# A look-ahead of seven groups in place of fourteen for the gathers of a three-layer graph network kernel

## The chip, the cores and the metric

One Trainium2 chip, one of its cores. The metric is the device time of one execution in microseconds (us), as the median of several runs. The engines are TensorE (PE), VectorE (DVE), ScalarE (ACT), GpSimd (POOL) and SyncE (SP). Every engine runs its own list of instructions; they meet at semaphores.

## The reference

A graph of 3125 nodes with 128 features and 53125 arcs (each node has one to itself; the kernel calls a node's number of arcs its degree) goes three times through this layer, and then through a last normalization:

```python
msg = concat([h[src], h[dst]]) @ Mw.T + Mb
s1, s2 = segment_sum(msg, dst), segment_sum(msg * msg, dst)
mx, mn = segment_max(msg, dst), segment_min(msg, dst)
mean = s1 / deg;  var = relu(s2 / deg - mean * mean);  std = sqrt(var + 1e-30)
agg = concat([mx, mn, std, var])
u = concat([h, agg, agg * (logd / 4), agg * (4 / logd)]) @ Uw.T + Ub
u = batch_norm(u / sqrt(N));  h = leaky_relu(u @ mix_w.T + mix_b) + h
h = elu(layer_norm(h))
...
out = layer_norm(x + h)
```

Only h[src] @ part of Mw has to be fetched for each arc. The kernel stores that product and its square, p and p*p, as a table in memory with one row of 1 KB for each node, and for each node gathers the rows of its sources, from which come sum, sum of squares, largest and smallest.

## The kernel before, in words

**Prologue.** Degrees are counted on TensorE, nodes are ranked by degree, and the indices of each node's sources are laid out by rank, so that each of the 25 tiles of 128 nodes has nodes of nearly one degree. The first table (`p_by_node`) is stored by node, and a second (`p_by_rank`) by rank. In `project(-1, c)` TensorE makes the products of seven chunks of four tiles (the last has one), VectorE adds the bias (L1440), ScalarE squares (L1058), and SyncE stores the chunk (L561). Before those stores SyncE issues 36 small transfers that fill `shared_index` (L557).

**Stage A of a layer** is where the change is. A slot is one gathered row for each of a tile's 128 nodes: one indirect DMA of GpSimd, of 128 rows (L742). Up to four slots are a group; `GROUPS` is the list of the 112 groups of a layer in order, and `own_slots[n]` says how many of group n's slots GpSimd gathers itself: 387 a layer, 1161 in all. Groups 0 to 3 (`AHEAD`) hold two slots for each of eight late tiles, 4 and 5 are tile 0, 6 to 8 tile 1, 9 to 11 tile 2, and so on. Before group 9, GpSimd gathers ten more sets of rows into `shared` (L727), out of which SyncE fills a few single slots by its own transfers (`shared_rows`, L564 to L585). Groups 26, 35 and 44 hold only such slots.

The gathered groups lie in a ring `G` of `R` = 14 places of four slots. Group n lies at place n % 14. Who uses a group:

- VectorE, `accumulate(l, n)`: adds, takes the larger and takes the smaller into PSUM, three instructions a group (L1470 to L1472). The last of them counts up `dve_used` ("groups_compared"). A tile's first group (j = 0) is copied by ScalarE instead (`begin`, L1101 to L1103), and is counted together with the tile's second. The AHEAD groups go into `base` (L1488 to L1490).
- ScalarE, in the first layer alone, `keep_ranks(l, n)` (L1091): writes the gathered rows' ranks back into `index`, and counts `rank_kept`.

At a tile's end VectorE reduces (`close`, L1692 to L1696), ScalarE squares the mean (`square_mean`, L1109), VectorE takes the variance (L1714), ScalarE the root (L1116), TensorE turns the aggregates (L921) and multiplies (L933, L936), ScalarE copies (L1129, L1135, L1141), and VectorE combines (L1722, L1724).

**What sets GpSimd's order.** `gather(l)` goes through the groups in order; its gathers are issued one after another and land by themselves. From group 14 on it first waits until VectorE has used the group that lay at this place, and in layer 0 until ScalarE has kept its ranks. GpSimd can thus be at most fourteen groups ahead. In layers 1 and 2 the first four groups wait for as many chunks of the new table as they need, and group 4 for all of it. Each further group wait on SyncE's side (L575) goes by R too.

**What VectorE waits for before its first group.** `take_ahead` waits for `base_ready`: ScalarE's `bases(l)` must have copied and scaled all tiles' own rows (L1075, L1077, and in layers 1 and 2 L1074), which begins when the last chunk has been squared. In layer 0 it waits also for the seven stores of `p_by_rank` (`s_firstp`).

**Stage B of a layer** (batch norm, mix, layer norm, ELU, next table) runs chunk by chunk on TensorE, ScalarE and VectorE, when the last tile is done. After layer 2 GpSimd scatters the outputs (L753).

Of the kernel before, what the change touches and what calls it, by code (L numbers as in the profile page):

```python
# [72 lines left out]
def build(nc, x, src, dst, w_p, b_p, w_q, w_h, w_u, w_mix, v_cols, out):  # L73
# [101 lines left out]
            GROUPS.append((T - 1, -1, 0, hi - lo))  # L175
    NG = len(GROUPS)
    R = 14
    W = 2 * D + 1
    slot_before, slot_total = [], [0] * R
    kept_to = [sum(k > 0 for k in own_slots[:n + 1]) for n in range(NG)]  # L180
    for n in range(NG):
        slot_total[n % R] += 16 * own_slots[n]
        slot_before.append(slot_total[n % R])
    tile_groups = [[n for n, g in enumerate(GROUPS) if g[0] == t and g[1] >= 0] for t in range(T)]
# [13 lines left out]
    with ctx:  # L198
        def sb(name, shape, dt=FP32):
            return ctx.enter_context(nc.sbuf_tensor(name, shape, dt))  # L200

        def sem(name):
            return ctx.enter_context(nc.semaphore(name))
# [4 lines left out]
        rank_dram = nc.dram_tensor("rows_by_rank", [NP, RW], FP32).ap()  # L208
        p0_table = nc.dram_tensor("p_by_node", [NP, W], FP32).ap()
        p_table = nc.dram_tensor("p_by_rank", [NP, 2 * D], FP32).ap()  # L210
# [36 lines left out]
        shared_index = sb("shared_index", [P, NOV, 2], I32)  # L247
        shared = sb("shared_rows", [P, NOV, W])
        rdeg = sb("rdeg", [P, T])
# [10 lines left out]

        G = sb("G", [P, R, GW, W])
        G_flat = G[:, :, :, :].rearrange("p r k f -> p (r k f)")

        def carver(flat, size):
            taken = [0]

            def carve(n):
                at = taken[0]
                taken[0] += n
                assert taken[0] <= size  # L270
                return flat[:, at:at + n]

            return carve
# [12 lines left out]

        carve = carver(G_flat, R * GW * W)
        hot_lo = carve(P * HC)[0:EP, :].bitcast(BF16).rearrange("p (b j c) -> p b j c", b=2, c=HC)
# [3 lines left out]
        digit_b = carve(EC)[0:EP, :].bitcast(BF16).rearrange("p (b c) -> p b c", b=2)  # L292
        carve = carver(G_flat, R * GW * W)
        p_nat = carve(T * W).rearrange("p (t f) -> p t f", f=W)
        rows_flat = carve(T * RW)
# [132 lines left out]
        dve_used = Signal(sem("groups_compared"), NG)  # L428
        rank_kept = Signal(sem("ranks_kept"), NG)
# [181 lines left out]
        def _(pool):  # L611
# [66 lines left out]
            def extras(l):  # L678

                with pool.If(pool.value_load(extra_i[0:1, T:T + 1], min_val=0, max_val=T * E) > 0):  # L680
                    with pool.Fori(0, T) as t:
                        more = pool.value_load(extra_i[0:1, bass.ds(t, 1)], min_val=0, max_val=T * E)
                        with pool.If(more > 0):
                            with pool.Fori(0, more):
                                pool.wait_ge(x_arc, 1)
                                pool.sem_clear(x_arc)
                                g.indirect_dma_start(ex_src[:, :], None,
                                                     src.rearrange("(e a) -> e a", a=1),
                                                     bass.IndirectOffsetOnAxis(ap=ex_arc[:, :], axis=0))\
                                    .then_inc(x_src, 16)  # L690
                                pool.wait_ge(x_node, 1)
                                pool.sem_clear(x_node)
                                g.indirect_dma_start(ex_row[:, :], None, p0_table,
                                                     bass.IndirectOffsetOnAxis(ap=ex_node[:, :], axis=0))\
                                    .then_inc(x_p, 16)
                                if l:
                                    pool.wait_ge(x_rank, 1)
                                    pool.sem_clear(x_rank)
                                    g.indirect_dma_start(ex_row[:, 0:2 * D], None, p_table,
                                                         bass.IndirectOffsetOnAxis(ap=ex_rank[:, :], axis=0))\  # L700
                                        .then_inc(x_q, 16)
                        pool.nop()
                    pool.nop()
                pool.nop()

            def gather(l):

                if l:
                    pool.wait_ge(s_need, 1)
                    needs = [pool.value_load(need_i[0:1, l - 1, a:a + 1], min_val=p_stored.at(l - 1, 16),  # L710
                                             max_val=p_stored.at(l - 1, 16 * NC)) for a in range(len(AHEAD))]
                for n, (t, ahead, k0, _) in enumerate(GROUPS):
                    table, w = (p_table, 2 * D) if l else (p0_table, W)
                    if l and n in AHEAD:
                        pool.wait_ge(p_stored.sem, needs[n])
                        pool.sem_inc(s_turn, 1)
                    elif n == len(AHEAD) and l == 0:
                        pool.wait_ge(s_infor, 80)
                    elif n == len(AHEAD):
                        pool.wait_ge(p_stored.sem, p_stored.at(l - 1, 16 * NC))  # L720
                    if n == tile_groups[2][0]:
                        if l == 0:
                            pool.wait_ge(s_sidx, 16 * len(PARTS))
                        if l == 1:
                            pool.wait_ge(s_skept, 1)
                        for c in range(NOV):
                            g.indirect_dma_start(shared[:, c, 0:w], None, table,  # L727
                                                 bass.IndirectOffsetOnAxis(ap=shared_index[:, c, 0:1], axis=0))\
                                .then_inc(shared_in.sem, 16)
                    if n == R:  # L730
                        if l == 0:
                            pool.wait_ge(s_extra, 1)
                            pool.sem_inc(s_turn, 1)
                        extras(l)
                    if n >= R:

                        pool.wait_ge(dve_used.sem, dve_used.at(l, n - R + 1))
                        if l == 0:
                            pool.wait_ge(rank_kept.sem, rank_kept.at(l, kept_to[n - R]))
                    for j in range(own_slots[n]):  # L740
                        named = index[:, t + j, k0:k0 + 1] if n in AHEAD else index[:, t, k0 + j:k0 + j + 1]
                        g.indirect_dma_start(G[:, n % R, j, 0:w], None, table,  # L742
                                             bass.IndirectOffsetOnAxis(ap=named, axis=0))\
                            .then_inc(gathered[n % R].sem, 16)
# [3 lines left out]
            for l in range(L):  # L748
                gather(l)
# [1122 lines left out]
```

## Time and profile before

| what | value |
|---|---|
| median of 3 runs | 1751.79 us (1750.67 to 1752.85) |
| span of the profiled execution | 2141.7 us |
| GpSimd busy, of the span | 1235.7 us (58%) |
| VectorE busy | 1096.6 us (51%) |
| TensorE busy (matmul) | 682.6 us (32%) |
| ScalarE busy | 455.6 us (21%) |
| gathers of L742 | 1161, 949 ns each |

The profiled execution is 389.9 us (22%) longer than the median of the timed runs; of its own time only the span is given. A busy share is the time in which instructions of that engine ran, out of the span. For GpSimd a gather's duration is the issue, and not the transfer, which goes on behind it. The stretches by layer, by the first and the last gather: layer 0 from 110.8 to 708.5 us, layer 1 from 784.0 to 1378.0, layer 2 from 1450.5 to 2029.4; what lies before is the prologue, between them stage B, and behind them stage B and the output.

### The profile page before, as it was taken

How to read it: one execution, taken by the hardware profiler on the slowest of the kernel's cores; microseconds unless marked ns; L12 is line 12 of the kernel's file. 1: busy time of each engine (PE TensorE's matmuls, PEld its weight loads, DVE VectorE, ACT ScalarE, POOL GpSimd, SP SyncE). 2: the span in 40 equal slices, each digit the busy share in tenths (PEclk: the TensorE clock that was granted, in tenths of full speed). 3: DMA queues.
4: the chain of work that ended last, by engine and by line, in shares of the span. 5: the costliest groups of instructions: out<-in, count | busy, mean ns of one | idle time of the engine just before them, and what ended most of it. 6: DMA issues, size and time to landing. Idle time of an engine off the chain costs nothing. (4 is left out here: it accounts for less than half of the span.)

```text
span 2141.7 us, 10446 instructions
## 1 busy us (share of the span) xinstructions
PE 682.6 (32%) x2156; PEld 402.8 (19%) x2156; DVE 1096.6 (51%) x2178; ACT 455.6 (21%) x1024; POOL 1235.7 (58%) x1358
## 2 busy tenths in 40 slices
PE   5611233132322470323132232362113322233265
PEld 5311121011111230112111111131101211112122
DVE  8600755464644843445464463572525664466464
ACT  0103321122111154111111111136101221112125
POOL 7673666676666127745675675406756666576504
PEclk9975666565655685566565666686556666656677
DMA  4363333333333033323332232204323333333200
GB/s 59 105 167 113 93 103 103 91 99 92 92 91 91 18 112 113 111 66 99 96 101 76 88 103 75 65 27 145 106 84 101 93 88 93 88 103 96 76 0 30
DMA packets 97107, 190.18 MB, mean 89 GB/s; under 512 B 30792, under 2 KB 56984, under 8 KB 97040
## 3 DMA queue, kind: packets, MB, share of 16 engines
q0 software_dynamic: 59968, 160.78, 26.6%
q1 hardware_dynamic: 37077, 28.77, 4.9%
q14 instruction: 47, 0.39, 0.1%
q8 instruction: 15, 0.25, 0.0%
HBM read 168.75 MB, written 17.75 MB: 87 GB/s over the span
## 5 line engine op out<-in xcount | busy, mean ns | idle before, releaser
L742 POOL DMA_INDIRECT G<-p_by_rank,index x774 | 734.8, 949 | 560.2 <-issue 227.8
L742 POOL DMA_INDIRECT G<-p_by_node,index x387 | 367.4, 949 | 225.0 <-issue 120.3
L921 PE MATMUL ps<-wide_ident,agg 128*128 128x128 f32 x288 | 80.3, 434 | 1209.3 <-issue 701.2
L1470 DVE TENSOR_TENSOR ps<-ps,G 128x1024 f32<-128x1024 f32 (+3 forms) x222 | 250.3, 1127 | 191.2 <-issue 78.4
L921 PEld LDWEIGHTS ps<-wide_ident,agg 128*128 128x128 f32 x288 | 51.5, 217 | 1239.5 <-issue 721.9
L936 PE MATMUL ps<-w_u_sb,aggT 128*128 128x384 f32 x576 | 284.3, 654 | 0.0
L1714 DVE SCALAR_TENSOR_TENSOR var<-tot,rdeg,msq 128x128 f32<-128x128 f32 x75 | 26.1, 348 | 426.4 <-ACT msq L1109 407.8
L936 PEld LDWEIGHTS ps<-w_u_sb,aggT 128*128 128x128 f32 x576 | 162.6, 282 | 144.7 <-issue 119.1
L1135 ACT ACTIVATE u_sb<-ps 128x128 f32<-128x128 f32 x75 | 20.7, 277 | 721.1 <-remote 509.0
L1472 DVE TENSOR_TENSOR ps<-ps,G 128x512 f32<-128x512 f32 (+3 forms) x222 | 141.6, 638 | 0.0
L1471 DVE TENSOR_TENSOR ps<-ps,G 128x512 f32<-128x512 f32 (+3 forms) x222 | 141.5, 637 | 0.0
L933 PE MATMUL ps<-w_own,hT 128*128 128x384 f32 x144 | 107.3, 849 | 4.1 <-remote 2.0
L1692 DVE TENSOR_REDUCE tot<-ps 128x256 f32<-128x1024 f32 x72 | 88.2, 1225 | 34.6 <-remote 21.6
L1129 ACT ACTIVATE aggT<-ps 128x512 f32<-128x512 f32 x72 | 42.3, 587 | 245.8 <-remote 171.7
L1109 ACT ACTIVATE msq<-tot,rdeg 128x128 f32<-128x128 f32 x75 | 29.8, 397 | 244.0 <-DVE tot L1692 177.3
L1101 ACT ACTIVATE ps<-G 128x1024 f32<-128x1024 f32 x72 | 72.8, 1011 | 1.8 <-issue 1.8
L753 POOL DMA_INDIRECT out_h<-G,index x25 | 24.8, 993 | 80.4 <-ACT G L1215 72.8
L1488 DVE TENSOR_TENSOR base<-base,G 128x1024 f32<-128x1024 f32 x12 | 14.8, 1233 | 76.9 <-remote 67.2
L1141 ACT ACTIVATE uT<-ps,v_sb 128x128 f32<-128x128 f32 x75 | 27.4, 365 | 115.2 <-remote 75.5
L839 PE MATMUL ps<-w_p_sb,hT 128*128 128x128 f32 x150 | 26.5, 331 | 77.4 <-issue 51.6
L1116 ACT ACTIVATE agg<-agg,eps_std 128x128 f32<-128x128 f32 x75 | 30.1, 401 | 90.2 <-DVE agg L1717 60.0
L1696 DVE TENSOR_REDUCE agg<-ps 128x128 f32<-128x512 f32 x72 | 49.0, 681 | 0.0
(280 smaller groups left out, 1328.3 us busy)
## 6 DMA issues: line engine op xcount, KB each, us to landing
G<-p_by_rank,index POOLq DMA_INDIRECT x774
p_by_rank<-base SPq DMA_DIRECT2D x18, 512.0 KB
G<-p_by_node,index POOLq DMA_INDIRECT x387
p_by_node<-G SPq DMA_DIRECT2D x6, 514.0 KB
w_u_sb<-in_w_u SPq DMA_DIRECT2D x3, 768.0 KB
x_r<-rows_by_rank SPq DMA_DIRECT2D x1, 1600.0 KB
G<-shared_rows SPq DMA_DIRECT2D x12, 53.0 KB
windows<-src_pad SPq DMA_DIRECT2D x1, 624.8 KB, 14.1
```

Of the source, the lines that this page charges most:

```text
L742: g.indirect_dma_start(G[:, n % R, j, 0:w], None, table, bass.IndirectOffsetOnAxis(ap=named, axis=0))\
L921: ins = nc.tensor.transpose(ps[:, 2, i * D:(i + 1) * D], agg[:, t % 2, i * D:(i + 1) * D], ident[:, :])
L933: mm(z, hT[:, hot(t)], w_own[:, :], start=True, stop=False)
L936: ins = mm(z, aggT[:, t % 2, i * D:(i + 1) * D], w_u_sb[:, i, :], start=False, stop=i == 3)
L1101: f(run, G[:, n % R, :, 0:2 * D], ACT.Copy)
L1116: f(agg[:, t % 2, 2 * D:3 * D], agg[:, t % 2, 3 * D:4 * D], ACT.Sqrt, bias=eps_std[:, 0:1]).then_inc(std_ready.sem, 1)
L1129: f(aggT[:, t % 2, :], ps[:, 2, :], ACT.Copy).then_inc(agg_copied.sem, 1)
L1470: TT(run[:, 0:nk, :], run[:, 0:nk, :], G[:, n % R, 0:nk, 0:2 * D], ALU.add)
L1471: TT(top[:, 0:nk, :], top[:, 0:nk, :], here, ALU.max)
L1472: TT(low[:, 0:nk, :], low[:, 0:nk, :], here, ALU.min).then_inc(dve_used.sem, 2 if j == 1 else 1)
L1692: sums = v.tensor_reduce(tot[:, t % 2, :], run.rearrange("p k f -> p f k"), AX.X, ALU.add)
L1696: least = v.tensor_reduce(agg[:, t % 2, D:2 * D], low.rearrange("p k d -> p d k"), AX.X, ALU.min)
```

## The change

GpSimd waits from group 7 on for the group seven back, in place of from group 14 on for the group fourteen back. The ring keeps its 14 places, and SyncE's wait for its own slots still goes by R.

```diff
     R = 14
+    LOOK = 7
...
-                    if n >= R:
-
-                        pool.wait_ge(dve_used.sem, dve_used.at(l, n - R + 1))
+                    if n >= LOOK:
+
+                        pool.wait_ge(dve_used.sem, dve_used.at(l, n - LOOK + 1))
                         if l == 0:
-                            pool.wait_ge(rank_kept.sem, rank_kept.at(l, kept_to[n - R]))
+                            pool.wait_ge(rank_kept.sem, rank_kept.at(l, kept_to[n - LOOK]))
```

No instruction of another engine moves or changes. On GpSimd waits are added at the start of each layer. The list of GpSimd at the start of layer 0's gathers, before; `G<-p_by_node,index` is a gather of L742, and the first two rows are groups 0 to 3, the next two groups 4 to 8:

```order
L742 DMA G<-p_by_node,index 128x257 [waits first_p_stored,indices_of_early_tiles_loaded]
L742 DMA G<-p_by_node,index 128x257 x15
L742 DMA G<-p_by_node,index 128x257 [waits indices_by_rank_loaded]
L742 DMA G<-p_by_node,index 128x257 x17
L727 DMA shared_rows<-p_by_node,shared_index 128x257 [waits shared_index_loaded]
L727 DMA shared_rows<-p_by_node,shared_index 128x257 x9
L742 DMA G<-p_by_node,index 128x257 x17
```

The same place with the change (line numbers are one higher):

```order
L743 DMA G<-p_by_node,index 128x257 [waits first_p_stored,indices_of_early_tiles_loaded]
L743 DMA G<-p_by_node,index 128x257 x15
L743 DMA G<-p_by_node,index 128x257 [waits indices_by_rank_loaded]
L743 DMA G<-p_by_node,index 128x257 x11
L743 DMA G<-p_by_node,index 128x257 [waits ranks_kept,groups_compared]
L743 DMA G<-p_by_node,index 128x257
L743 DMA G<-p_by_node,index 128x257 [waits ranks_kept,groups_compared]
L743 DMA G<-p_by_node,index 128x257 x3
L728 DMA shared_rows<-p_by_node,shared_index 128x257 [waits shared_index_loaded]
L728 DMA shared_rows<-p_by_node,shared_index 128x257 x9
L743 DMA G<-p_by_node,index 128x257 [waits ranks_kept,groups_compared]
L743 DMA G<-p_by_node,index 128x257 x3
```

The first wait for VectorE and ScalarE stands now behind 28 gathers (16 and 12) instead of behind 51 gathers and the ten of L728, and the ten stand behind two such waits.

The start of layer 1, with the change; before, the row x11 was x17 and led without a wait up to the ten shared gathers:

```order
L743 DMA G<-p_by_rank,index 128x256 [waits p_stored]
L743 DMA G<-p_by_rank,index 128x256 x11
L743 DMA G<-p_by_rank,index 128x256 [waits groups_compared]
L743 DMA G<-p_by_rank,index 128x256
L743 DMA G<-p_by_rank,index 128x256 [waits groups_compared]
L743 DMA G<-p_by_rank,index 128x256 x3
L728 DMA shared_rows<-p_by_rank,shared_index 128x256 [waits shared_ranks_kept]
```

Here too group 7 is the first that waits for VectorE, and no wait for ScalarE stands beside it.

## Rows read from the trace of the kernel before

**Rows 1.** The page: span, busy time by engine, and the groups of line 742.

```profile
span 2141.7 us, 10446 instructions
PE 682.6 (32%) x2156; PEld 402.8 (19%) x2156; DVE 1096.6 (51%) x2178; ACT 455.6 (21%) x1024; POOL 1235.7 (58%) x1358
...
L742 POOL DMA_INDIRECT G<-p_by_rank,index x774 | 734.8, 949 | 560.2 <-issue 227.8
L742 POOL DMA_INDIRECT G<-p_by_node,index x387 | 367.4, 949 | 225.0 <-issue 120.3
```

**Rows 2.** Who waited for whom, GpSimd: us in total, times, longest us.

```profile
POOL G L742 <- DVE ps L1472: 175.2, 23, 23.2
...
POOL G L742 <- ACT index L1091: 77.6, 9, 32.7
POOL G L742 <- DVE ps L1587: 23.0, 2, 11.6
```

**Rows 3.** Timeline, GpSimd: start us, us, instruction, [idle before <-releaser].

```profile
110.80 0.99 POOL L742 DMA_INDIRECT G<-p_by_node,index  x1 [7.18 <-DMA index<-rows_by_rank]
...
145.87 0.94 POOL L742 DMA_INDIRECT G<-p_by_node,index  x1 [0.30 <-issue]
...
219.48 1.69 POOL L742 DMA_INDIRECT G<-p_by_node,index  x1 [32.66 <-ACT index L1091]
...
707.58 0.94 POOL L742 DMA_INDIRECT G<-p_by_node,index  x1 [2.22 <-DVE ps L1472]
...
783.97 1.11 POOL L742 DMA_INDIRECT G<-p_by_rank,index  x1 [75.45 <-DMA p_by_rank<-base]
...
819.14 0.94 POOL L742 DMA_INDIRECT G<-p_by_rank,index  x1 [0.31 <-issue]
...
1377.10 0.94 POOL L742 DMA_INDIRECT G<-p_by_rank,index  x1 [8.26 <-DVE ps L1472]
...
2028.48 0.94 POOL L742 DMA_INDIRECT G<-p_by_rank,index  x1 [0.52 <-DVE ps L1472]
```

**Rows 4.** Timeline, VectorE: first and last use of gathered groups in a layer.

```profile
216.78 1.23 DVE L1488 TENSOR_TENSOR base<-base,G 128x1024 f32<-128x1024 f32 x1 [9.68 <-ACT base L1077]
...
750.68 0.28 DVE L1583 TENSOR_TENSOR agg<-ps,G 128x128 f32<-128x128 f32 x1
...
836.69 1.23 DVE L1488 TENSOR_TENSOR base<-base,G 128x1024 f32<-128x1024 f32 x1 [34.30 <-remote]
...
1418.90 0.28 DVE L1583 TENSOR_TENSOR agg<-ps,G 128x128 f32<-128x128 f32 x1
...
2070.71 0.28 DVE L1583 TENSOR_TENSOR agg<-ps,G 128x128 f32<-128x128 f32 x1
```

**Rows 5.** Who waited for whom, VectorE's largest.

```profile
DVE var L1714 <- ACT msq L1109: 407.8, 29, 27.4
```

**Rows 6.** Timeline, ScalarE, the bases of layer 1.

```profile
810.16 1.82 ACT L1077 ACTIVATE base<-base,self_w 128x256 f32<-128x256 f32 x4
...
817.77 0.51 ACT L1077 ACTIVATE base<-base,self_w 128x256 f32<-128x256 f32 x1 [0.89 <-issue]
```

**Rows 7.** Timeline, VectorE, a tile of four groups in layer 2: its start, the next one's.

```profile
1872.24 1.23 DVE L1470 TENSOR_TENSOR ps<-ps,G 128x1024 f32<-128x1024 f32 x1 [1.68 <-ACT ps L1103]
...
1886.00 1.23 DVE L1470 TENSOR_TENSOR ps<-ps,G 128x1024 f32<-128x1024 f32 x1 [1.65 <-issue]
```

**Rows 8.** Timeline, VectorE, chunks of the table: layer 0, and the last one before layer 1.

```profile
127.11 0.69 DVE L1440 TENSOR_TENSOR base<-ps,b_p_sb 128x512 f32<-128x512 f32 x1 [8.72 <-issue]
156.41 0.69 DVE L1440 TENSOR_TENSOR base<-ps,b_p_sb 128x512 f32<-128x512 f32 x1 [28.61 <-remote]
...
196.38 0.69 DVE L1440 TENSOR_TENSOR base<-ps,b_p_sb 128x512 f32<-128x512 f32 x1 [6.37 <-remote]
...
200.29 0.89 DVE L1440 TENSOR_TENSOR base<-ps,b_p_sb 128x512 f32<-128x512 f32 x2 [1.23 <-PE ps L839]
...
799.28 0.29 DVE L1440 TENSOR_TENSOR base<-ps,b_p_low 128x128 f32<-128x128 f32 x1 [0.89 <-issue]
```

**Rows 9.** Timeline, SyncE's transfers in the prologue.

```profile
117.23 0.44 SPq L551 DMA_DIRECT2D v_sb<-in_v_cols  x1
117.72 35.15 SPq L557 DMA_DIRECT2D shared_index<-rows_by_rank  x36
```

## The prediction

> **What bounds the kernel now.** I read the page first, then GpSimd's waits, then the timelines of GpSimd and VectorE at the seams of the layers. On the page GpSimd is the busiest engine, and its gathers are 949 ns each [rows 1]. They do not follow at 949 ns: the 28 gathers from 110.80 to 145.87 us took 35.07 us, 1.25 us each, and the group's "issue" share (348.1 us of idle time before 1161 gathers, 0.30 each) is the rest of it [rows 1, 3]. The same 1.25 us stands wherever GpSimd waits for nobody. With the ten shared gathers a layer there are 3 x 397 = 1191 of them: 1489 us of GpSimd.
>
> In the profiled execution GpSimd has waits on top of that: 175.2 + 77.6 + 23.0 = 275.8 us for a ring place, released by VectorE or ScalarE [rows 2]. And VectorE is far behind: it ends its last group 43.4, 42.1 and 42.5 us after the last gather of the layer was issued [rows 3, 4]. If VectorE were close behind, some 5 us would do for the issue, the landing and the last use (an estimate: 0.94 for the issue, about 1 for the last three instructions, the rest for the landing). Three times 37.5 is 112 us. Both together, 388 us, are what the profiled execution has over a kernel that only gathers at 1.25 us without a pause. Its span is 389.9 us over the median of the timed runs: 2141.7 - 388 = 1753.7 against 1751.79.
>
> From this I take that the timed runs have none of those waits: there GpSimd issues from a layer's start to its end, and VectorE follows. VectorE can: its whole busy time is 1096.6 us [rows 1], and a tile of four groups, 15 gathers or 18.8 us of GpSimd, costs it 13.8 us when nothing holds it [rows 7]. What holds it in the profile is a stretch in which the other engines are served slowly while GpSimd gathers. ScalarE does four scalings in 1.82 us at 810.16, and from 812.9 on each of the same takes a turn of 1.40 us (0.51 busy, 0.89 "issue") [rows 6]; VectorE's 407.8 us for the squared mean are the same thing further down the chain [rows 5]. These stretches are in the profile; by the sum above they are not in the timed runs. The Trainium skill, page "NOTIFIC — the notification-queue block", section 3, says that the unit that writes trace records can push back on the engines that produce them and so stall one; no run here shows that this is the cause.
>
> **The change, part by part.**
>
> 1. *Removed:* nothing. *Added:* 28 waits in the list of GpSimd (seven more groups a layer, on two semaphores in layer 0). A wait that is already met costs nothing here: gathers with and without one before them start 1.25 us apart [rows 3]. I take 0; an upper bound of 0.02 us each is under 1 us.
>
> 2. *Start of layer 0.* GpSimd starts at 110.80 and has issued groups 0 to 6, 28 gathers, when it comes to group 7 at 145.87 [rows 3]. With the change it stands there until VectorE has used group 0 and ScalarE has kept its ranks. In the profile that is 219.48, but only because of the slow stretch: chunk 0 of the table passed VectorE at 127.11, chunk 1 at 156.41, and then, when GpSimd had paused, the chunks from 196.38 to the last (end 201.18) took 4.8 us for three steps [rows 8]. Two steps of those are 200.29 - 196.38 = 3.9 us. Without a slow stretch the six steps from 127.11 are 3 x 1.95 + 4.8 = 10.7 us, and the last chunk is through at about 137.8. From there to the first use of a gathered group it is 216.78 - 201.18 = 15.6 us (ScalarE's table load and its bases) [rows 4, 8]: 153.4. From the start of that use to GpSimd's next gather it is 219.48 - 216.78 = 2.7: 156.1. The other path is SyncE's: 36 small transfers at the 0.49 us between its rows, 17.6 us, end at 135.3 [rows 9]; the seven stores behind them then go out as their chunks come, and land beside the 15.6 us of the bases. So GpSimd stands still from 145.87 to 156.1, 10.2 us. The contention of the stores with the gathers and the first keeping of ranks will add a little; I take 12. What is queued behind the wait is everything: 23 gathers of groups 7 to 13 and the ten shared ones, 41.3 us of issue, that were already under way before. Since GpSimd sets the end of the layer, those 12 us are not given back.
>  Bounds: below, 0, if VectorE were ready by 145.87; above, 30. For that the slow stretch is there until GpSimd stops at 145.87; after it chunk 1 passes at some 147, the five steps to the last are 2 x 1.95 + 4.8 = 8.7 us, then come 15.6 and 2.7: 174, or 28 us.
>
> 3. *Start of layers 1 and 2.* Group 7 comes at 819.14, 35.2 us after the layer's first gather [rows 3]. The last chunk passed VectorE at 799.57 [rows 8]. From there it is layer 0's 15.6 us again, with one more copy a chunk (seven of some 0.6) and without the table load (some 1.3): 18.5, an estimate; then 2.7 give 820.8, and without the slow turns before 799.28 about 3 us less. A wait of 0 to 2 us each; I take 0. At the profile's own slow values it would be 836.69 + 2.7 - 819.14 = 20 us each.
>
> 4. *In the middle of the layers.* Seven places hold at least 16 gathers of GpSimd's own (13 where the group waited for is counted with the next one), 16 to 20 us. A wait there needs VectorE to be that far behind the landing. With the tail of a tile (13.8 less three groups of 2.5, about 6 us), a group of its own and the four single slots of a shared group, I come to at most some 17, and that only behind the nine shared groups. I take 0, and an upper bound of 1 us at each of the nine shared groups.
>
> Sum: 12 us over the profiled execution's figure without its waits, and so over the median: 1751.8 + 12 = 1764.
>
> **A rule that speaks for more.** The profile shows 34 ring waits, and they come back every 60 us or so [rows 2]. The Trainium skill, page "Perfetto Trace Analysis", section "Optimization Strategy", says that a gap which repeats on the engine that should be saturated can mean too few buffers. By that rule halving the lead would lengthen each gap; by the sum above there are none in timed runs to lengthen. It is the second rival.
>
> **The rivals.**
>
> - *A, the forecast:* one stop, at layer 0's start. 1757 to 1774. Chance 0.55.
> - *B, more stops:* the repeating gaps are real, in part. VectorE is as late at the starts as the profile has it, or nearly: 30 us in layer 0, and up to 20 in layers 1 and 2. From 1782 with the first alone up to 1822 with all three. For it speaks every timeline of the profile; against it that GpSimd's 1489 us and the 246 us before, between and behind the layers' uses (110.8, 33.0, 31.3 and 70.7) leave only 17 us of the median, landings included. Chance 0.2.
> - *C, nothing:* VectorE's chain, and not GpSimd, ends the layers, so that a lead of gathers that are lost at the start is not missed, or VectorE is ready before 145.87. For it speaks that in the profile VectorE is 42 us late at every end. 1751 to 1754. Chance 0.17.
> - *D, faster:* the slow stretch while GpSimd gathers is in the timed runs too, and VectorE's chain sets the end. Then the stop at 145.87 ends the slow stretch 41 us earlier than before (GpSimd's last gather before its pause began at 185.9), and VectorE begins layer 0 at 172 in place of 216.78: up to 45 us off, 1707. It decides from the point where VectorE is still more than a few us behind at 707.58, the layer's last gather. Half of the saving, lost again to a thinner lead, would be 1730. Chance 0.08.
>
> That the change would not do what it says is excluded by the list of instructions: group 7 waits in every layer.
>
> **How the numbers follow.** The likeliest case gives 1764. Its own range is 1757 to 1774. The range for 8 in 10 takes in case C and B's first step: 1751 to 1788; what is left out is D and the upper half of B, some 0.18. A measurement of this kernel can tell about 0.2%, 3.5 us, from no change. The chance of over 0.2% faster is D's, 0.08; of within 0.2% C's, 0.17; of over 0.2% slower A's and B's, 0.75.
>
> **What would show it.** In the profile with the change GpSimd's 29th gather has a gap before it that ends with VectorE's first L1491 or ScalarE's L1092, and VectorE's first use of a group lies at 150 to 180, not at 216.78. Its ring waits will be more than 34, and the longest no longer 32.7. GpSimd's pace between waits stays at 1.25 us. The timed difference should lie near 12 us and not near 40 to 70. I am wrong if the timed runs are within 3.5 us, or if they are over 1785; the first would say that GpSimd is not what ends layer 0, the second that VectorE falls back by more than 16 gathers in timed runs too.

## The result, and the profile after

| | time |
|---|---|
| before, 12 runs | 1750.34 us (1746.51 to 1752.85) |
| after, 12 runs | 1753.37 us (1752.11 to 1756.52) |
| ratio | 1.0024, 95% interval 1.0016 to 1.0032 |

The medians lie 3.0 us apart; the ratio, which uses all runs, gives 4.2 us, with an interval of 2.8 to 5.6. The forecast was 12 (1764.0, with a range of 1751 to 1788): the sign was right, the size was three to four times too large.

The page of the profiled execution after, which answers to [rows 1]:

```profile
span 1750.9 us, 10453 instructions
...
PE 670.2 (38%) x2156; PEld 394.9 (23%) x2156; DVE 1094.0 (62%) x2178; ACT 456.0 (26%) x1024; POOL 1236.1 (71%) x1358
...
L743 POOL DMA_INDIRECT G<-p_by_rank,index x774 | 736.2, 951 | 307.0 <-issue 232.4
...
L743 POOL DMA_INDIRECT G<-p_by_node,index x387 | 367.4, 949 | 128.4 <-issue 113.9
```

The busy times of VectorE, ScalarE and GpSimd are those of before within 2.6 us, and TensorE's is 12 us less, but the span is 390.8 us shorter. That is not the change: this time the profiled execution looks like the timed ones (1750.9 beside 1753.37). The slow stretches of rows 5 and 6 are gone: ScalarE's four scalings of a chunk take 1.69 us from the first to the last, and the wait for the squared mean is no longer among VectorE's largest. GpSimd's waits show the same, to be held against [rows 2] (us in total, times, longest):

```profile
POOL G L743 <- issue: 346.3, 1137, 0.3
POOL G L743 <- DMA p_by_rank<-base: 71.8, 2, 36.8
...
POOL G L743 <- DVE base L1491: 6.5, 1, 6.5
...
POOL G L743 <- DVE ps L1473: 3.7, 12, 0.3
```

The 34 ring waits of 275.8 us are one of 6.5 us. Every other gather has the 0.30 us before it that it has without a wait; the second row is the two starts of layers 1 and 2.

The one stop is where the prediction put it. GpSimd's timeline (start us, us, instruction, idle before and its releaser), at the seams of the layers:

```profile
108.22 0.99 POOL L743 DMA_INDIRECT G<-p_by_node,index  x1 [4.62 <-DMA index<-rows_by_rank]
...
142.22 0.94 POOL L743 DMA_INDIRECT G<-p_by_node,index  x1 [0.30 <-issue]
149.71 1.68 POOL L743 DMA_INDIRECT G<-p_by_node,index  x1 [6.55 <-DVE base L1491]
...
610.99 0.94 POOL L743 DMA_INDIRECT G<-p_by_node,index  x1 [0.30 <-DVE ps L1588]
...
647.02 1.10 POOL L743 DMA_INDIRECT G<-p_by_rank,index  x1 [35.09 <-DMA p_by_rank<-base]
...
682.88 1.63 POOL L743 DMA_INDIRECT G<-p_by_rank,index  x1 [0.30 <-issue]
...
1144.00 0.94 POOL L743 DMA_INDIRECT G<-p_by_rank,index  x1 [0.30 <-DVE ps L1588]
...
1679.16 0.95 POOL L743 DMA_INDIRECT G<-p_by_rank,index  x1 [0.30 <-DVE ps L1588]
```

The 29th gather starts at 149.71 instead of at 143.46: 6.25 us of stop. In layer 1 the same gather comes at 682.88 with no stop. VectorE, in the same stretches, beside [rows 4] and [rows 8]:

```profile
122.18 0.69 DVE L1441 TENSOR_TENSOR base<-ps,b_p_sb 128x512 f32<-128x512 f32 x1 [5.96 <-PE ps L840]
124.16 0.69 DVE L1441 TENSOR_TENSOR base<-ps,b_p_sb 128x512 f32<-128x512 f32 x1 [1.29 <-PE ps L840]
125.50 0.69 DVE L1441 TENSOR_TENSOR base<-ps,b_p_sb 128x512 f32<-128x512 f32 x1 [0.64 <-PE ps L840]
...
129.16 0.89 DVE L1441 TENSOR_TENSOR base<-ps,b_p_sb 128x512 f32<-128x512 f32 x2 [0.31 <-PE ps L840]
...
147.01 1.23 DVE L1489 TENSOR_TENSOR base<-base,G 128x1024 f32<-128x1024 f32 x1 [11.08 <-DMA p_by_rank<-base]
...
677.55 1.23 DVE L1489 TENSOR_TENSOR base<-base,G 128x1024 f32<-128x1024 f32 x1 [14.86 <-ACT base L1078]
...
1148.39 0.28 DVE L1584 TENSOR_TENSOR agg<-ps,G 128x128 f32<-128x128 f32 x1
...
1683.47 0.28 DVE L1584 TENSOR_TENSOR agg<-ps,G 128x128 f32<-128x128 f32 x1
```

Two things are to be seen. The last chunk is through at 130.05, and the first use of a group starts at 147.01, 38.8 us after the first gather; in the profiled execution of before it was 106.0 us after it (216.78 - 110.80). And VectorE begins its last group of layers 1 and 2 now 4.4 and 4.3 us after the last gather began (1148.39 - 1144.00 and 1683.47 - 1679.16), where before it was 42 us in both.

### The profile page after: what moved, and what is told of

Its sections match the earlier page's. It is cut to its first block and busy times, and to the rows that moved or that the text cites. A ratio compares the mean times of both kernels' runs of the same rounds, so it can differ in the third digit from the quotient of the medians.

```text
span 1750.9 us, 10453 instructions
## 1 busy us (share of the span) xinstructions
PE 670.2 (38%) x2156; PEld 394.9 (23%) x2156; DVE 1094.0 (62%) x2178; ACT 456.0 (26%) x1024; POOL 1236.1 (71%) x1358
## 5 line engine op out<-in xcount | busy, mean ns | idle before, releaser
L937 PE MATMUL ps<-w_u_sb,aggT 128*128 128x384 f32 x576 | 277.4, 641 | 0.0
L937 PEld LDWEIGHTS ps<-w_u_sb,aggT 128*128 128x128 f32 x576 | 158.8, 276 | 141.5 <-issue 113.1
L1472 DVE TENSOR_TENSOR ps<-ps,G 128x512 f32<-128x512 f32 (+3 forms) x222 | 141.3, 637 | 0.0
L1092 ACT ACTIVATE index<-G 128x4 int32<-128x4 f32 (+2 forms) x108 | 21.1, 202 | 187.2 <-DMA G<-p_by_node,index 187.2
L1697 DVE TENSOR_REDUCE agg<-ps 128x128 f32<-128x512 f32 x72 | 49.0, 680 | 0.0
L1695 DVE TENSOR_REDUCE agg<-ps 128x128 f32<-128x512 f32 x72 | 48.9, 680 | 0.0
L665 POOL DMA_INDIRECT base<-windows,row_i x25 | 37.5, 1501 | 13.7 <-issue 7.3
L1103 ACT ACTIVATE ps<-G 128x512 f32<-128x512 f32 x72 | 42.1, 585 | 0.0
```

The lines of the kernel that those rows point to most:

```text
L937: ins = mm(z, aggT[:, t % 2, i * D:(i + 1) * D], w_u_sb[:, i, :], start=False, stop=i == 3)
L1103: f(top, G[:, n % R, :, 0:D], ACT.Copy)
L1472: TT(top[:, 0:nk, :], top[:, 0:nk, :], here, ALU.max)
L1695: most = v.tensor_reduce(agg[:, t % 2, 0:D], top.rearrange("p k d -> p d k"), AX.X, ALU.max)
L1697: least = v.tensor_reduce(agg[:, t % 2, D:2 * D], low.rearrange("p k d -> p d k"), AX.X, ALU.min)
```

## The experiments

"Theory 1" in the expectations is the prediction's view with the sizes of the trace after: timed runs have no slow stretch, GpSimd's unbroken issue sets the time, and a shorter look-ahead costs its stops at the starts of the layers and nothing between them. Line numbers of a kernel with the extra lines are one higher than before, in mid3 two.

### Was the slow stretch in the kernel or in one execution?

**look14** is the kernel before, unchanged, profiled again.

> The kernel before, unchanged, for a second profile of it and for the noise of a comparison. Theory 1 (GpSimd's issue at 1.25 us a gather bounds every timed run; the stretches of slow service belonged to that one profiled execution): the span is 1746 to 1752 us, no ring wait before any gather, VectorE's first use of a group in layer 0 at 147 to 151 us, ratio 1.000. Theory 2 (a lead of fourteen groups makes the slow stretches in every profiled execution): the span is again near 2140 us with some 276 us of ring waits, ratio 1.000.

Measured: 1749.44 us beside 1749.73 for before, ratio 1.0004 (0.9992 to 1.0016). Its page, and then GpSimd's waits:

```profile
span 1747.0 us, 10446 instructions
...
PE 658.7 (38%) x2156; PEld 387.7 (22%) x2156; DVE 1094.2 (63%) x2178; ACT 456.6 (26%) x1024; POOL 1238.3 (71%) x1358
```

```profile
POOL G L742 <- issue: 349.8, 1148, 0.3
...
POOL G L742 <- ACT index L1091: 1.2, 4, 0.3
...
POOL G L742 <- DVE ps L1472: 0.9, 3, 0.3
```

The same kernel, 394.7 us shorter, and no ring wait of more than the 0.3 us of issue. Theory 1 had that right, but not VectorE's first use in layer 0: it comes at 145.15, ahead of the 147 to 151 expected. So rows 2 to 6 described one execution and not the kernel. None of the other profiles below has a slow stretch either. From here on look14 stands for the profile of before.

### Which of the added waits costs?

**only_start** has the look-ahead of seven only in layer 0's groups 7 to 13, **not_start** everywhere else.

```diff
 only_start
+                    back = LOOK if l == 0 and n < R else R
 not_start
+                    back = R if l == 0 and n < R else LOOK
 both
-                    if n >= LOOK:
-                        pool.wait_ge(dve_used.sem, dve_used.at(l, n - LOOK + 1))
+                    if n >= back:
+                        pool.wait_ge(dve_used.sem, dve_used.at(l, n - back + 1))
```

> The look-ahead of seven only in layer 0 for groups 7 to 13; fourteen elsewhere. Theory 1 (the whole price is the one stop at layer 0's group 7): same as the changed kernel, 1753 us, +2 to +4 us over before, with one ring wait of 6 to 7 us. Rival (the price is spread over the layers, in waits too short to be seen): 1750 to 1751 us.

> The look-ahead of seven everywhere but for groups 7 to 13 of layer 0. Theory 1: same as before, 1750 us, within 1 us, and no ring wait over 0.5 us. Rival (spread over the layers): +2 to +3 us.

Measured: only_start 1753.49, ratio 1.0018 (1.0006 to 1.0030); not_start 1750.97, ratio 1.0008 (0.9997 to 1.0018), both beside 1749.73. only_start has one stop, of 4.8 us where 6 to 7 were expected, and not_start none:

```profile
147.83 1.68 POOL L743 DMA_INDIRECT G<-p_by_node,index  x1 [4.79 <-DVE base L1491]
```

So the waits of layer 0's groups 7 to 13 alone cost what the whole change costs. All the other places have the shorter look-ahead in not_start, and its ratio is not distinct from 1. By the times alone they could still cost up to 3.2 us, and its median is 1.2 us up where within 1 was expected; that they cost nothing is shown by its trace, in which no gather waits for a place.

### Does the price follow the stop?

**look9**, **look6** and **look5** set `LOOK` to nine, six and five.

> Look-ahead nine in every layer. Theory 1 (the price of a look-ahead is its stop at the layers' starts, and nothing in mid-layer): the first wait stands at group 9, behind the ten shared gathers, some 57 us after the layer's first gather, when VectorE has used more than group 0 (its use ends 41 us after it in layer 0, 36 us in layers 1 and 2). No ring wait over 0.5 us, span 1745 to 1749, the median within 2 us of before's 1750. Rival (a thinner lead costs all along the layers, by late landings): about two thirds of what seven costs, 2.5 us, so 1752 to 1753.

> Look-ahead six in every layer. Theory 1: the wait at group 6 comes 3 to 5 us earlier than the one at group 7, with VectorE as late as before: stops of 10 to 11 us in layer 0 and of 3 to 4 us in each of layers 1 and 2, together 16 to 19, of which 1 to 3 come back as shorter waits behind VectorE's first instructions: a median of 1765 to 1768. Rival (only layer 0's start costs, and the other two starts have room): 10 us, 1760.

> A look-ahead of five. Theory 1, from the profile of the changed kernel: group 5 comes after 20 gathers, 25 us after a layer's first; VectorE has used group 0 at 149.4, 680.0 and 1213.9 us there, so the stops are 16, 8 and 7 us, 31 in all; with the 3 us that were missing at seven, 1778 us (1.016). If a stop is given back in about half wherever it is, 1766 us. If VectorE in the middle of a layer is further behind than five groups, there are more stops and it is over 1785 us.

Measured: look9 1749.0, ratio 1.0000 (0.9989 to 1.0010), no stop; look6 1761.57, ratio 1.0063 (1.0047 to 1.0079); look5 1778.6, ratio 1.0156 (1.0138 to 1.0174). The stops of the last two, GpSimd's waits in look6 and its timeline in look5:

```profile
POOL G L743 <- ACT index L1092: 11.9, 5, 10.6
...
POOL G L743 <- DVE base L1491: 3.4, 2, 2.7
```

```profile
148.11 1.68 POOL L743 DMA_INDIRECT G<-p_by_node,index  x1 [14.95 <-DVE base L1491]
...
690.22 1.69 POOL L743 DMA_INDIRECT G<-p_by_rank,index  x1 [7.25 <-DVE base L1491]
...
1231.91 1.69 POOL L743 DMA_INDIRECT G<-p_by_rank,index  x1 [7.92 <-DVE base L1491]
```

look9 and look5 came as theory 1 had it. look6 missed its 1765 to 1768 by 3.4 us and lay nearer to the rival's 1760: its stop in layer 0 is the expected 10.6, but those of layers 1 and 2 are 0.7 and 2.7, of which 0.3 is the normal gap, in place of 3 to 4. The rival's reason (the other two starts have room) is nevertheless wrong, since they do stop; they stop less. In layer 1 VectorE's first use comes 29.0 us after the first gather, 1.5 sooner than in after, and a gather of 1.95 us just ahead of the stop took 1.0 us of it, which the next experiment explains.

### What shortens a stop again?

In look14 the gathers beside VectorE's first instructions are not all of 0.95 us. GpSimd, then VectorE, in the same few microseconds:

```profile
145.85 1.35 POOL L742 DMA_INDIRECT G<-p_by_node,index  x1 [0.30 <-issue]
147.50 0.95 POOL L742 DMA_INDIRECT G<-p_by_node,index  x1 [0.31 <-issue]
148.75 1.43 POOL L742 DMA_INDIRECT G<-p_by_node,index  x1 [0.30 <-issue]
150.49 1.63 POOL L742 DMA_INDIRECT G<-p_by_node,index  x1 [0.30 <-issue]
```

```profile
145.15 1.23 DVE L1488 TENSOR_TENSOR base<-base,G 128x1024 f32<-128x1024 f32 x1 [9.69 <-ACT base L1077]
146.29 0.68 DVE L1489 TENSOR_TENSOR base<-base,G 128x512 f32<-128x512 f32 x1
...
147.50 1.26 DVE L1488 TENSOR_TENSOR base<-base,G 128x1024 f32<-128x1024 f32 x1
148.68 0.68 DVE L1489 TENSOR_TENSOR base<-base,G 128x512 f32<-128x512 f32 x1
149.28 0.68 DVE L1490 TENSOR_TENSOR base<-base,G 128x512 f32<-128x512 f32 x1
...
150.09 1.21 DVE L1488 TENSOR_TENSOR base<-base,G 128x1024 f32<-128x1024 f32 x1
151.22 0.68 DVE L1489 TENSOR_TENSOR base<-base,G 128x512 f32<-128x512 f32 x1
```

Take 0.95 us back from the end of each long gather: 146.25, 149.23 and 151.17, each 0.04 or 0.05 before VectorE's next instruction begins. They look held until the instruction in which they started is over: each ends 0.82 us after that instruction's end (147.20 after 146.38, 150.18 after 149.36, 152.12 after 151.30). The gather that starts together with one, at 147.50, is not held. In the eleven profiles without a slow stretch it is the same each time: 108 gathers begin at least 0.06 us inside one of the three and more than 0.14 us before its end, and all end 0.81 or 0.82 us after it; 47 begin within 0.04 us of its start, and none is held. Four gathers a layer are held in look14. Over all gathers longer than 0.96 us, what they take beyond 0.946 us (the excess, below) is 7.2 us in look14 and 6.0 in after. **light14** and **light7** are the kernels before and after without the sum and the maximum of the four early groups (two of the three instructions; their results are missing from eight tiles).

```diff
-                TT(sums, sums, G[:, n % R, :, 0:2 * D], ALU.add)
-                TT(most, most, here, ALU.max)
                 TT(least, least, here, ALU.min).then_inc(dve_used.sem, 1)
```

> The kernel before, with the sum and the maximum of the four early groups left out (their minimum alone is taken, one instruction of 0.69 us a group in place of three of 2.6). Theory P (a gather that starts while one of those instructions with both operands in SBUF runs is held until it ends: the 12 gathers of 1.35 to 1.69 us at the starts of the layers, 6.1 us over the 0.95 in all, are that): at most 0.5 us a layer of such excess is left, and the span falls by 4.5 to 6.5 us from the 1747.0 of the kernel before, to 1740.5 to 1742.5; median near 1745. Rival (the long gathers come from other traffic, such as the landing of the first transfers or SyncE's stores): the excess stays near 2 us a layer and the span near 1747.

> The same leaving out, with the look-ahead of seven. Theory P with theory 1: VectorE has used group 0 some 1.9 us sooner, so the one stop is 2.9 to 4.7 us (in place of 4.8 to 6.5), and since there are no held gathers that a stop could spare, all of it is lost: span 3 to 4.7 us over that of the same kernel with fourteen. Rival (what a stop loses comes back by some other way, as 1.3 to 2.6 us of it did with the full kernel): 1 to 2.5 us over it.

Measured, beside 1750.45: light14 1743.79, ratio 0.9967 (0.9956 to 0.9977), light7 1746.31, ratio 0.9979 (0.9968 to 0.9989). The excess is 1.8 us in light14 instead of 7.2 (0.5 to 0.7 a layer, where at most 0.5 was expected); the median fell by 6.7 us (4.0 to 7.7 by the interval). The long gathers went with the instructions, so they are VectorE's doing. The expected span, 1740.5 to 1742.5, was missed: 1745.4. Of the 5.4 us less of excess only 2.9 show in the sum of the 1191 gathers' durations (1134.0 to 1131.1), since the other gathers of that one execution were 2 ns longer each; look9's are 2 ns longer than look14's as well, though nothing there should change them, and the median of ten runs is the better witness. In light7 the stop is 3.1 us over the normal gap:

```profile
146.64 1.15 POOL L743 DMA_INDIRECT G<-p_by_node,index  x1 [3.44 <-DVE base L1489]
```

light7's median is 2.5 us above light14's, which is the upper end of the rival's 1 to 2.5. The expectation of 3 to 4.7 was for spans, and light7's span is even 1.6 us the shorter one: single spans scatter by more than what was to be told apart here. So theory P is borne out by light14, and whether something else gives part of a stop back is not settled by light7.

The Trainium skill, page "SBUF — State Buffer", section "SBUF: two separate sides", says that VectorE and GpSimd share a pair of ports which an instruction of VectorE with two inputs in SBUF can hold for its whole length against a GpSimd instruction that reads SBUF. The trace agrees: L1488 to L1490 have both inputs in SBUF, and a gather that starts inside one ends 0.82 us after it. L1470 to L1472 have one input in PSUM and run 222 times each; 398 gathers of look14 begin while one of them runs, and none takes over 0.96 us. Of the few others that are long, the first of layer 1 (1.09 us) and one in the middle of layer 2 (1.06) began inside instructions with all inputs in SBUF too (L1807, L1714), and they too end 0.82 us after them.

### What lies between the stop of 4.8 and that of 6.5?

In after VectorE's first use was released by the last store of `p_by_rank`, at 147.01, 1.4 us after ScalarE's last base (145.62). **stores_first** is the changed kernel with SyncE's seven stores ahead of the 36 small transfers.

```diff
-            sp.wait_ge(s_cleared, 1)
-            for t, _, lo, hi, q, c, o in PARTS:
...
             for c, (t0, nt) in enumerate(CH):
                 sp.wait_ge(p_copied.sem, p_copied.at(-1, c + 1))
                 sp.dma_start(p_table[t0 * P:(t0 + nt) * P, :].rearrange("(t p) f -> p t f", p=P),
...
+            sp.wait_ge(s_cleared, 1)
+            for t, _, lo, hi, q, c, o in PARTS:
```

> The changed kernel, with SyncE's seven stores of the table by rank ahead of the 36 small transfers. In the profile of the changed kernel VectorE's first use was released at 147.01 by the last of these stores, 1.4 us behind ScalarE's last base (145.62); in the one with seven at the start alone both came at 145.0 to 145.1. Theory S (the store is the later of the two in some executions and makes the stop 6.5 in place of 4.8): the first use is released by ScalarE's base, at 145.0 to 146.0, the stop is 4.7 to 5.7 us and the median falls by 0 to 1.5 us from 1753.4. Rival (the store comes late because of the gathers' traffic, and not because of its place in SyncE's list): it is still the store that releases VectorE, at 146 or later.

Measured: 1753.57, ratio 1.0020 (1.0010 to 1.0029). VectorE's first use and GpSimd's stop:

```profile
144.93 1.23 DVE L1489 TENSOR_TENSOR base<-base,G 128x1024 f32<-128x1024 f32 x1 [9.69 <-ACT base L1078]
```

```profile
147.63 1.69 POOL L743 DMA_INDIRECT G<-p_by_node,index  x1 [4.70 <-ACT index L1092]
```

As theory S had it for the trace: ScalarE's base releases VectorE and the stop is 4.7. But one profile can't show that the order did it, since six of the ten undisturbed profiles with the old order have ScalarE as the releaser too. In those ten, VectorE's first use comes 36.8 to 39.0 us after the first gather. The store is the last to come in four of them, and late by over 1 us in two, after and look9 (38.8 and 39.0); the other eight lie at 36.8 to 37.8, most of which spread is the time between the first two chunks (1.2 to 2.5 us). With the 2.7 us from there to the next gather, and GpSimd's 35.2, the ten would make stops of 4.3 to 6.5 us, 4.9 in the middle (an estimate from these rows). The median did not move by anything that can be measured, so the longer stop is not in most timed runs, or its 1.5 us are too few to see.

### Is the middle of the layers free at any look-ahead?

**mid3** leaves groups 7 to 13 alone and waits from group 14 on for the group three back.

```diff
-                    if n >= LOOK:
+                    back = R if n < R else 3
+                    if n >= back:
```

> A look-ahead of three in the middle of the layers alone: groups 14 and up wait for the group three back, groups 7 to 13 for none. From the table of when each group was gathered and used in the profile of the same kernel with fourteen: with seven, six or five no group of the middle would have to wait, with four one or three a layer, with three 17 or 18 a layer. Theory 1 (the middle costs nothing at seven because VectorE is there never more than some 14 us behind, and starts to cost where the lead falls under that): ring waits of 95 us in all if each stop also delays the uses behind it, 19 us if it delays none; a median of 1769 to 1845, and above 1765 in any case. Rival (GpSimd's gathers are hidden in mid-layer and VectorE's own work sets the pace there): under 5 us, 1755 or less.

Measured: 1839.38 us, ratio 1.0515 (1.0498 to 1.0531), 89.0 us over before. GpSimd's waits:

```profile
POOL G L744 <- DVE ps L1474: 57.5, 33, 4.9
POOL G L744 <- DVE ps L1589: 42.5, 15, 5.4
```

With ScalarE's, 46 stops of 88.0 us over the normal gap. The 95 expected if each stop also delays the uses behind it came from look14's trace, from a table of when each group was gathered and used. So the middle is not free by nature; at seven it is free because VectorE is never so far behind that group n - 7 is still in use when GpSimd comes to group n.

### All together

Stops are the idle time before gathers over the normal 0.30 us, in one profiled execution; excess is that of the long gathers, against look14's 7.2; the last column is the median's difference from before in the same series, in us.

| kernel | stops | excess against look14 | sum | measured |
|---|---|---|---|---|
| light14 | 0 | -5.4 | -5.4 | -6.7 |
| light7 | 3.1 | -4.9 | -1.8 | -4.1 |
| look9 | 0 | 0.0 | 0.0 | -1.5 |
| not_start | 0 | -1.0 | -1.0 | +1.2 |
| only_start | 4.5 | -0.1 | 4.4 | +3.8 |
| stores_first | 4.4 | -0.8 | 3.6 | +3.2 |
| after | 6.2 | -1.2 | 5.0 | +3.0 |
| look6 | 13.1 | -1.3 | 11.8 | +11.1 |
| look5 | 29.2 | -2.3 | 26.9 | +28.9 |
| mid3 | 88.0 | +0.9 | 88.9 | +89.0 |

Over a range of 90 us the stops and the held gathers account for the time within 2.4 us. Effects smaller than that this table can't tell apart: not_start has 1.0 us less excess than look14 without any stop.

## Why the prediction was right in sign and three to four times too large

**What bounds the kernel: right.** "GpSimd issues from a layer's start to its end" in timed runs was worked out from a profile that showed the opposite, as 2141.7 - 388 = 1753.7. look14 shows it directly: span 1747.0, no ring wait. The 1.25 us a gather stands in every profile, and longer stops lengthen the time one for one (look6, look5, mid3).

**Part 1, waits that are met cost 0: right.** look9 and not_start.

**Part 2, one stop in layer 0: right in place and releaser, wrong in size.** In time after the first gather:

| step | predicted | after |
|---|---|---|
| GpSimd comes to group 7 | 35.1 | 35.2 |
| first chunk at VectorE | 16.3 | 14.0 |
| from there to the end of the last chunk | 10.7 | 7.9 |
| last chunk to first use | 15.6 | 17.0 (15.6 in look14) |
| first use to the next gather | 2.7 | 2.7 |
| GpSimd goes on | 45.3 | 41.5 |
| stop | 10.2 | 6.2 |

The step that failed is "the six steps from 127.11 are 3 x 1.95 + 4.8 = 10.7", and its starting point. Both were read from rows 8. The starting point lies in the slow stretch: the chunk at 127.11 has "8.72 <-issue" ahead of it, and 16.3 us after the first gather became 14.0. The steps of 1.95 lie behind it, in GpSimd's pause (its last gather before that began at 185.9), and there VectorE waited for TensorE ("1.23 <-PE ps L839" in rows 8). The eight products of a chunk, in before and in after:

```profile
196.26 2.08 PE L839 MATMUL ps<-w_p_sb,hT 128*128 128x128 f32 x8 [25.77 <-ACT hT L1063]
```

```profile
124.40 1.06 PE L840 MATMUL ps<-w_p_sb,hT 128*128 128x128 f32 x8
```

In before TensorE had stood idle for 25.77 us, and its granted clock was 0.50 from 196 to 200 us, the 1.2 GHz level; in after it was at work since 118.11, and the clock was 1.00 from 124 to 131, the 2.4 GHz level. So behind the idle stretch the products took twice as long, and the steps read there were 1.95, where all eleven undisturbed profiles have 1.33 for the second to the fourth step (124.16, 125.50 above). The first step is of another size, 1.98 in after. Together it is 5.2 us too many (2.4 for the starting point, 2.8 for the steps), of which 1.4 came back by the late store. The prediction had SyncE's stores land beside the bases; in after the last of them landed 1.4 us behind. The two intervals that were copied whole, 15.6 and 2.7, were exact but for that store (15.6 in look14). Then "the contention ... will add a little; I take 12" added 1.8 for what was 1.4 in this execution, 0.1 in only_start and 0 in stores_first.

**"Those 12 us are not given back": not refuted, and not shown to the last us.** The stop falls where VectorE holds gathers: in layer 0 two are held by its first instructions in place of four. From the first to the last gather layer 0 takes 5.3 us more than in look14 (502.8 against 497.5), for a stop of 6.2; its excess is 0.7 us less. The excess of all three layers is 1.2 us less, but 0.5 of that is in layer 1, which has no stop, and not_start shows the like without any. 6.2 - 1.2 = 5.0 is inside the interval of 2.8 to 5.6 and near the ratio's 4.2, and an estimate with the middle stop of 4.9 and the 0.7 of layer 0 is 4.2 too. That the medians give only 3.0 is not explained; at this look-ahead, with VectorE's work whole, three profiles show a stop, 6.2 once and 4.4 and 4.5 in the two variants.

**Part 3, layers 1 and 2: right.** "0 to 2 us each; I take 0": in layer 1 VectorE ends group 0 at 679.98, 33.0 us after the first gather, and group 7 comes 35.9 after it. The prediction's 820.8 was 36.8 us after the layer's first gather; by the rows it would be 30.5 + 2.7 = 33.2, and of the 3.6 too many it named about 3 itself. Less than 3 us of room is left: at six both layers stop, at five by 7.3 and 7.9.

**Part 4, mid-layer: right.** not_start for seven; mid3 shows that it is a matter of size.

**The rule that spoke for more** (repeating gaps on the engine that should be saturated, the Trainium skill, page "Perfetto Trace Analysis", section "Optimization Strategy"): the gaps of rows 2 were in the profiled execution alone, so there was nothing to lengthen. The measurement decides against it here.

**The rivals.** A happened, one stop at layer 0's start, but below its own 1757 to 1774. B and D both rested on the slow stretch being in timed runs, which look14 excludes. C (1751 to 1754) held the measured 1753.37, but for reasons that aren't there: GpSimd does stop, and the layers' ends follow it (VectorE is 4 to 5 us behind, not 42).

**The signs it named.** The gap before the 29th gather and its releaser came as said. VectorE's first use was to lie at 150 to 180 and lay at 147.01, and the ring waits were to be more than 34 and were one. "I am wrong if the timed runs are within 3.5 us": the medians are 3.0 apart, so by its own sign it was wrong. But what that was to mean, "that GpSimd is not what ends layer 0", is not what the runs show; the stop was small.

What wrote the slow stretch into the first profile is not known; no kernel here reproduced it in eleven profiles.

## What to carry to other kernels

When a profiled execution is far longer than the timed runs, work out first which waits the timed runs can't contain, and then distrust every interval inside the disturbed stretch, and the steps right behind it too: here whole intervals behind a dependency (15.6, 2.7) held to 0.1 us where no store came late, and the short steps were read a third to a half too long (10.7 for 7.9, 1.95 for 1.33), since TensorE came out of an idle stretch at the lower clock. A second profile of the unchanged kernel is worth more than either. In this kernel a look-ahead costs its stops, one for one to within 2.4 us, since its engine sets the time, and nothing until the consumer's largest lag exceeds it; that lag is at the start of a layer, and a table of "gathered at, used at" for each group tells it, and also how steeply the price rises below it (seven 3 to 4 us, six 11, five 29).

## What the runs showed of the hardware

A gather of GpSimd that starts inside a VectorE instruction with both inputs in SBUF is held until this is over, and ends 0.82 us after it: 0.95 us becomes up to 1.97. One that starts together with such an instruction is not held. Twelve instructions a layer do most of it, two to four gathers a layer are held by them, and taking eight of the twelve away made the kernel 6.7 us (4.0 to 7.7) faster. With one input in PSUM nothing of the kind is seen (398 gathers, none over 0.96 us). A version that keeps the whole result and takes the early groups' sums with one input in PSUM wasn't tried.

After 25.77 us of idle time TensorE's eight products of a chunk took 2.08 us, at a granted clock of 0.50 (1.2 GHz), and 1.06 us in the midst of its work at 1.00 (2.4 GHz).

One profiled execution of an unchanged kernel had a span 390 us longer than the median of its timed runs, and another of the same kernel one 2 us shorter.
